# Macaron block on one core: where POOL issues the gathers of the expert stage, and what they wait for

## Chip, core and metric

One Trainium2 chip, one core. The metric is the time of one execution on the device in microseconds (us). The engines are PE (matrix products), DVE (vector), ACT (activations), POOL (GpSimd) and SP (SyncE, which here only issues DMAs); each runs its own instructions in order, and they wait for one another through semaphores.

## What is computed

Input x is 8 x 512 tokens of 128 floats. The block is a macaron: half a mixture-of-experts layer, attention, half a mixture-of-experts layer again.

```python
x = x + 0.5 * ffn(layernorm(x))          # pass 1
x = x + attention(layernorm(x))          # 16 heads, softmax, projection, residual, layernorm
x = x + 0.5 * ffn(layernorm(x))          # pass 2

def ffn(x):                              # 4096 tokens, 64 experts, top 8, at most 64 tokens an expert
    probs = softmax(x @ router_w.T)
    topk_w, topk_ids = top_k(probs, 8);  topk_w /= topk_w.sum(-1)
    # x_buf[e, c] = the c-th token that chose expert e (tokens past 64 are dropped)
    h = silu(x_buf @ w_gate) * (x_buf @ w_up)
    y = h @ w_down
    routed = segment_sum(y[slot] * topk_w, token)
    shared = (silu(x @ ws_gate) * (x @ ws_up)) @ ws_down
    return routed + shared
```

## The kernel before

The 4096 tokens are 32 tiles of 128 (NT), taken in 8 groups of 4 (NG = 8, GT = 4). Each pass of the mixture layer is one call of `ffn(f)` on every engine (f.p is 0 in pass 1 and 1 in pass 2), and runs through these stages.

**Routing.** Per group the tokens are normalised, the router's product is made, and the weights of the top 8 experts are computed. Rows of the normalised token and its 64 weights (192 floats) go to DRAM (`dispatch_rows`); the waits `xns` and `ws` are for these stores.

**Shared expert.** Per group PE makes the up products, ACT copies them, POOL multiplies them (`shared_mul`, L589 to L593), PE makes the down product, ACT copies it (`shy`), and DVE adds it to x in place (`shared_add`, L859, semaphore `shx`). SP stores the sum to DRAM, group by group (`store_base`, L406, semaphore `base`): this is the base to which the experts' outputs are added.

**Lists.** DVE finds for each expert its tokens, in two halves: the first 32 slots of all 64 experts while the shared expert runs, the second 32 slots in between steps 0 to 3 of the expert loop (`merge_blocks`, `open_blocks`, `top_tokens`, `indices`). SP stores each list (L410) and loads it back spread over all partitions (L414), in eight parts.

**Experts.** 16 steps q, each with two tiles of 128 slots (k = 2q and 2q + 1; one tile is the 32 slots of four experts). POOL gathers the 128 rows of a tile with an indirect DMA (`gather(k)`, L599) into one of 16 buffers; PE transposes them (`slots_t`), makes the gate and up products (`gate_up`, semaphore `gu`), transposes the hidden values (`hidden_t`), makes the down product (`down_e`), and in `sums` adds up rows of the same token within the step. DVE finds which slots hold the same token (`match`), picks the routing weights (`pick`), multiplies gate and up (`hidden`, L914) and copies the sums out of PSUM (`sum_copy`, L922, semaphore `smc`). POOL then adds the sums to the base in DRAM with two indirect DMAs (L626, "scatter" below, semaphore `sca`).

Three rules of order matter here. A pair of scatters starts when both the sums are copied and the pair before has landed. `sum_copy(q)` waits until the pair of step q - 2 has landed. And a gather into a buffer used before waits until its transposes and its `pick` are done (k at 16 or more).

POOL's order before: the shared products of groups 0 to 5, gathers 0 and 1, the product of group 6, gather 2, the product of group 7, gathers 3 to 5, then waits for all base stores and for the second gate and up product (`wait(pool, f.gu, 2)`, L616), gathers 6 to 9, and then step by step a pair of scatters and the gathers up to `ahead(q + 1)`, where `ahead(q)` is 10 + 2q, at most 32.

SP's order in pass 1: the stores of the weights mixed with the 24 loads of expert weights, 13 loads of the attention's weights (`attention_weights`), the first list's store and first load, eight base stores, then the other list loads, each when the transposes have come so far (`gtp`). In pass 2 no weights are loaded. POOL waits for the attention's weights after it has cleared buffers behind the last scatter of pass 1.

Of the kernel before, what the change touches and what calls it, by code (L numbers as in the profile page):

```python
# [15 lines left out]
def macaron_kernel(nc, x_in, wq, bq, wk, bk, wv, bv, wo, bo, gamma, beta,  # L16
# [13 lines left out]
    NP2 = E // 2  # L30
# [31 lines left out]
    with ExitStack() as ctx:  # L62
# [292 lines left out]
        def _(sp):  # L355
# [6 lines left out]
            def attention_weights():  # L362
                sp.dma_start(wv_sb[:], wv).then_inc(s_watt, 16)
                sp.dma_start(wo_sb[:], wo.rearrange("(j d) n -> d j n", d=HD)).then_inc(s_watt, 16)
                for i, (w, b) in enumerate(((wq, bq), (wk, bk))):
                    sp.dma_start(wqk_raw[:, i * D:(i + 1) * D], w).then_inc(s_watt, 16)
                    sp.dma_start(bqk_sb[:, i:i + 1], b.rearrange("(j d o) -> d j o", d=HD, o=1), allow_slow_non_contiguous=True).then_inc(s_watt, 16)
                for jj in range(4):
                    sp.dma_start(bv_sb[jj * 32:(jj + 1) * 32, :].rearrange("p (k d) -> p k d", k=4),
                                 bv.rearrange("(o k jj d) -> jj o k d", o=1, k=4, jj=4)[jj].to_broadcast([32, 4, HD]))\  # L370
                      .then_inc(s_watt, 16)
                for t, b in ((bo_sb, bo), (gamma_sb, gamma), (beta_sb, beta)):
                    sp.dma_start(t[:], b.rearrange("(o c) -> o c", o=1).to_broadcast([P, D])).then_inc(s_watt, 16)
# [6 lines left out]
            def ffn(f):  # L380
# [6 lines left out]
                if f.p == 0:  # L387
                    for g in range(NG):
                        if g:
                            store_w(g - 1, (g - 1) % 2)  # L390
                        expert_weights(2 * g)
                        expert_weights(2 * g + 1)
                    store_w(NG - 1, 1)
                    for c in range(2 * NG, 24):
                        expert_weights(c)
                    attention_weights()
                else:
                    store_w(0, 0)
                    with sp.Fori(1, NG // 2) as i:
                        for r in range(2):  # L400
                            store_w(2 * i + (r - 1), 1 - r)
                    store_w(NG - 1, 1)
# [16 lines left out]
                for g in range(NG):  # L419
                    store_base(g, g % 2)  # L420
                for c in range(1, 4):
                    wait(sp, f.gtp, 2 * c - 1)
                    load_rows(c)
                store_list(1)
# [94 lines left out]
        def _(pool):  # L519
# [40 lines left out]
            def ffn(f):  # L560
# [43 lines left out]
                for r in range(2):  # L604
                    wait(pool, f.xns[r], 16 * (NG // 2))
                    wait(pool, f.ws[r], 16 * (NG // 2))
                for k in range(2):
                    gather(k)
                shared_mul(NG - 2, 0)
                gather(2)  # L610
                shared_mul(NG - 1, 1)
                for k in range(3, 6):
                    gather(k)
                for r in range(2):
                    wait(pool, f.base[r], 16 * (NG // 2))
                wait(pool, f.gu, 2)  # L616
                ahead = lambda q: min(NP2, 10 + 2 * q)
                for k in range(6, ahead(0)):
                    gather(k)
                for q in range(NQ):  # L620
                    wait(pool, f.row, q + 1)
                    wait(pool, f.smc, q + 1)
# [93 lines left out]
        def _(dve):  # L716
# [18 lines left out]
            def ffn(f):  # L735
# [191 lines left out]
                top_blocks(1)  # L927
                for g in range(5, NG):
                    shared_add(g)
                match(0)  # L930
                pick(0)
                hidden(0)
                match(1)
                pick(1)
                for q in range(NQ):
# [302 lines left out]
        def _(pe):  # L1238
            def ffn(f):
# [124 lines left out]
                      .then_inc(f.sm.sem, 1)  # L1364

                wait(pe, f.shc, NG)
                wait(pe, f.shy, NG)
                slots_t(0)
                gate_up(0)
                slots_t(1)  # L1370
                hidden_t(0)
                for q in range(NQ):
                    if q + 1 < NQ:
# [163 lines left out]
```

## Time and profile before

| | us |
|---|---|
| median of 3 runs | 892.09 |
| lowest and highest | 890.61, 896.19 |
| the profiled execution | 889.63 |
| its span in the trace | 887.9 |

The page of that execution gives these busy times in its span: PE 680.9 us (77%), DVE 604.6 (68%), ACT 464.8 (52%), POOL 391.1 (44%). They are averages over stages: the attention lies in the middle and keeps PE and DVE busy, the mixture layer stands before and behind it. A row of a timeline has the start in us from the span's start, the duration in us, the engine, the line of the kernel, the operation, what it writes and reads, how many instructions are merged in the row, and in brackets how long the engine had been idle and what released it. The duration of an indirect DMA on POOL is the time in which POOL makes its descriptors; the data land later. Where an instruction waits for several semaphores, the releaser named is the one that the profile saw last and can be another than the one that held it.

### The profile page before, as it was taken

The page shows a single profiled execution, that of the slowest core. Times are in us where ns is not written, and L with a number is a line of the kernel's source. Part 1 is how long each engine was busy: PE and PEld are TensorE (multiplying, and loading weights), DVE is VectorE, ACT ScalarE, POOL GpSimd, SP SyncE. Part 2 cuts the span into 40 slices and gives each one's busy share as a digit, 9 for nine tenths or more (in the row PEclk, how much of TensorE's full clock was granted, in tenths as well). Part 3 has the DMA queues.
Part 4 walks back from the last instruction along what each step waited for, and adds up shares of the span by engine and source line. Part 5 has one row for each costly group of instructions (what it writes and reads, how often), then busy time and mean ns, then how long its engine had stood idle before and what let it go on. Part 6 is the DMA issues. An engine that isn't in the chain of part 4 may idle for free. (4 is left out here: it accounts for less than half of the span.)

```text
span 887.9 us, 17088 instructions
## 1 busy us (share of the span) xinstructions
PE 680.9 (77%) x5121; PEld 313.0 (35%) x5121; DVE 604.6 (68%) x1572; ACT 464.8 (52%) x1060; POOL 391.1 (44%) x509
## 2 busy tenths in 40 slices
PE   4876765703899999999999999999980289676650
PEld 3643443502133333333333333333210264354440
DVE  4868643344978888888888888888913669864420
ACT  5733232201177777777777777777772675323210
POOL 5545887676432332322322322321004745677762
PEclk9987577555599999999999999999995559757665
DMA  6996443243525444445445445445110131644334
GB/s 186 256 240 174 79 76 58 38 91 67 97 50 96 89 88 95 87 86 95 85 88 95 83 90 95 81 92 95 38 36 18 36 89 25 170 83 77 50 33 107
DMA packets 233724, 80.26 MB, mean 90 GB/s; under 512 B 166888, under 2 KB 226440, under 8 KB 233608
## 3 DMA queue, kind: packets, MB, share of 16 engines
q1 hardware_dynamic: 212936, 64.94, 33.6%
q0 software_dynamic: 12288, 10.49, 8.0%
q10 hardware_dynamic: 8448, 4.20, 1.6%
q8 instruction: 25, 0.41, 0.2%
q14 instruction: 27, 0.22, 0.1%
HBM read 49.94 MB, written 31.49 MB: 92 GB/s over the span
## 5 line engine op out<-in xcount | busy, mean ns | idle before, releaser
L987 DVE TENSOR_REDUCE arena<-psum 128x2 f32<-128x1024 f32 x256 | 308.8, 1219 | 53.2 <-PE psum L1434 50.2
L1206 ACT ACTIVATE arena<-psum 128x512 f32<-128x512 f32 x512 | 282.1, 600 | 116.3 <-PE psum L1447 114.8
L1434 PE MATMUL psum<-arena 126*128 126x512 bf16 x512 | 200.1, 398 | 4.0 <-DVE arena L987 3.2
L1447 PE MATMUL psum<-arena 128*128 128x512 bf16 x512 | 196.8, 387 | 7.3 <-ACT arena L1206 3.3
L1456 PE MATMUL psum<-arena 128*32 128x512 f32 x1024 | 136.2, 604 | 0.3
L682 POOL CAST arena<-arena 128x256 bf16<-128x256 f32 x32 | 12.7, 397 | 265.0 <-issue 261.0
L626 POOL DMA_INDIRECT sums<-sums_sb,sidx x64 | 103.3, 1614 | 42.0 <-DVE sums_sb L922 18.6
L1447 PEld LDWEIGHTS psum<-arena 128*128 128x128 bf16 x512 | 50.7, 100 | 150.2 <-ACT arena L1206 122.3
L599 POOL DMA_INDIRECT arena<-dispatch_rows,arena x64 | 66.3, 1036 | 33.2 <-issue 17.4
L922 DVE COPY sums_sb<-psum 128x256 f32<-128x256 f32 x32 | 13.6, 424 | 97.0 <-DMA sums<-sums_sb,sidx 78.1
L1434 PEld LDWEIGHTS psum<-arena 126*128 126x128 bf16 x512 | 49.6, 99 | 37.9 <-DVE arena L987 15.1
L1319 PE MATMUL psum<-ident,arena 128*128 128x128 f32 x64 | 22.0, 390 | 34.9 <-DMA arena<-dispatch_rows,arena 33.1
L1244 PE MATMUL psum<-ident,xn_sb 128*128 128x128 f32 x64 | 17.8, 433 | 39.1 <-ACT xn_sb L1083 39.1
L1329 PE MATMUL psum<-wgu_sb,arena 128*32 128x192 f32 x512 | 41.7, 467 | 0.9 <-ACT arena L1144 0.9
L1150 ACT ACTIVATE arena<-psum 128x192 f32<-128x192 f32 x32 | 10.6, 330 | 59.5 <-PE psum L1329 59.5
L1456 PEld LDWEIGHTS psum<-arena 128*32 128x32 f32 x1024 | 20.3, 108 | 53.6 <-issue 29.1
L1339 PE MATMUL psum<-ident,arena 128*96 128x128 f32 x64 | 18.5, 385 | 24.3 <-DVE arena L914 24.1
L1396 PE MATMUL psum<-ident,arena 128*128 128x128 f32 x32 | 11.2, 348 | 32.0 <-POOL arena L667 32.0
L1083 ACT ACTIVATE xn_sb<-x_sb,negm,rstd 128x128 f32<-128x128 f32 x64 | 26.4, 491 | 16.8 <-DVE negm L739 15.5
L1176 ACT ACTIVATE arena<-psum 128x128 f32<-128x128 f32 x32 | 8.7, 273 | 48.4 <-PE psum L1396 48.4
L1144 ACT ACTIVATE arena<-psum 128x256 f32<-128x256 f32 x32 | 12.3, 383 | 40.5 <-PE psum L1319 40.4
L1000 DVE RECIPROCAL arena<-arena 128x128 f32<-128x128 f32 x32 | 30.1, 942 | 4.3 <-DMA arena<-ctx 4.3
(138 smaller groups left out, 1115.6 us busy)
## 6 DMA issues: line engine op xcount, KB each, us to landing
arena<-qk_parts SPq DMA_DIRECT2D x128, 96.0 KB
ctx<-arena SPq DMA_DIRECT2D x32, 256.0 KB, 2.0
qk_parts<-arena SPq DMA_DIRECT2D x32, 192.0 KB, 3.8
dispatch_rows<-xn_sb ACTq DMA_DIRECT2D x16, 256.0 KB, 2.3
arena<-lists SPq DMA_DIRECT2D x16, 256.0 KB, 3.5
sums<-x_sb SPq DMA_DIRECT2D x16, 256.0 KB, 4.4
arena<-qk_parts SPq DMA_DIRECT2D x64, 64.0 KB
arena<-ctx SPq DMA_DIRECT2D x64, 64.0 KB, 2.5
```

What stands on the lines that cost most here:

```text
L599: pool.indirect_dma_start(out=gat[k % NGB], out_offset=None, in_=xw_dram[f.p], in_offset=bass.IndirectOffsetOnAxis(ap=gidx[:, k:k + 1], ax ...
L626: pool.indirect_dma_start(out=acc_dram[f.p], in_=sum_r[q % 2][:, j * D:(j + 1) * D], in_offset=None, out_offset=bass.IndirectOffsetOnAxis( ...
L987: dve.tensor_reduce(mx_r[r % 2][:, 2 * p:2 * p + 2], src, X, ALU.max).then_inc(a_mx, 1)
L1000: dve.reciprocal(den2_r[r % 2], den2_r[r % 2]).then_inc(a_rc, 1)
L1083: ins = act.activation(xn_sb[:, r, j, :], x_sb[:, t, :], ACT.Identity, scale=rstd[:, t:t + 1], bias=negm[:, t:t + 1])
L1206: act.activation(p_r[tau % NPB], bank[4 + tau % 2][:, :], ACT.Exp, scale=SCALE).then_inc(a_P, 1)
L1319: ins = pe.transpose(bank[0][:, j * P:(j + 1) * P], gat[k % NGB][:, 0:D], ident[:])
L1329: ins = pe.matmul(bank[2 + r][i * HC:(i + 1) * HC, j * 2 * F:(j + 1) * 2 * F], gT[r][:, j * P + i * HC:j * P + (i + 1) * HC], wgu_sb[:, e, :],
L1339: ins = pe.transpose(bank[4][0:F, j * P:(j + 1) * P], hid[r][:, j * F:(j + 1) * F], ident[:])
L1434: ins = pe.matmul(bank[tau % 4][:, :], heads(q_st[r], rows, g)[:, qt * P:(qt + 1) * P], heads(k_st[r], rows, g), start=True, stop=True)
L1447: pe.matmul(bank[4 + tau % 2][:, :], keys, heads(q_st[r], rows, g), start=True, stop=True)\
L1456: ins = pe.matmul(bank[6][32 * g:32 * g + 32, :], v_r[r][:, g, kt, :], p_r[(4 * kt + g) % NPB], start=(kt == 0), stop=(kt == 3), tile_posi ...
```

## The change

- POOL: gathers and the last two shared products alternate (gather 0, product 6, gather 1, product 7), and then gathers 2 to 15 follow in a row. The wait for the second gate and up product is gone. The wait for the base stores stands behind these gathers, ahead of the first scatter. `ahead(q)` becomes 8 + 2q, at least 16 and at most 32: steps 0 to 3 have no gathers behind their scatters, steps 4 to 11 have two each.
- SP: the attention's weights are loaded between the first and the second of the list loads that wait for transposes, not ahead of the first list's store.
- DVE: `hidden(0)` comes before `match(0)` and `pick(0)`.
- PE: the wait for the last copy of the shared output stands ahead of the first hidden transposes, not ahead of the first slot transposes.

```diff
@@ SP
                     for c in range(2 * NG, 24):
                         expert_weights(c)
-                    attention_weights()
@@ SP
                 for c in range(1, 4):
+                    if c == 2 and f.p == 0:
+                        attention_weights()
                     wait(sp, f.gtp, 2 * c - 1)
                     load_rows(c)
@@ POOL
-                for k in range(2):
-                    gather(k)
+                gather(0)
                 shared_mul(NG - 2, 0)
-                gather(2)
+                gather(1)
                 shared_mul(NG - 1, 1)
-                for k in range(3, 6):
+                ahead = lambda q: min(NP2, max(16, 8 + 2 * q))
+                for k in range(2, ahead(0)):
                     gather(k)
                 for r in range(2):
                     wait(pool, f.base[r], 16 * (NG // 2))
-                wait(pool, f.gu, 2)
-                ahead = lambda q: min(NP2, 10 + 2 * q)
-                for k in range(6, ahead(0)):
-                    gather(k)
@@ DVE
+                hidden(0)
                 match(0)
                 pick(0)
-                hidden(0)
                 match(1)
@@ PE
                 wait(pe, f.shc, NG)
-                wait(pe, f.shy, NG)
                 slots_t(0)
                 gate_up(0)
                 slots_t(1)
+                wait(pe, f.shy, NG)
                 hidden_t(0)
```

POOL's rows from the first six shared products (TENSOR_TENSOR of 96 x 512) into the expert loop; the DMA rows that read `dispatch_rows` are gathers, those that write `sums` are scatters. Before:

```order
L593 TENSOR_TENSOR arena<-arena 96x512 x6
L599 DMA arena<-dispatch_rows,arena 128x192 x2
L593 TENSOR_TENSOR arena<-arena 96x512
L599 DMA arena<-dispatch_rows,arena 128x192
L593 TENSOR_TENSOR arena<-arena 96x512
L599 DMA arena<-dispatch_rows,arena 128x192 x7
L626 DMA sums<-sums_sb,sidx 8448x128 x2
L599 DMA arena<-dispatch_rows,arena 128x192 x2
```

The same place in the changed kernel, where the lines have moved by a few numbers:

```order
L594 TENSOR_TENSOR arena<-arena 96x512 x6
L600 DMA arena<-dispatch_rows,arena 128x192
L594 TENSOR_TENSOR arena<-arena 96x512
L600 DMA arena<-dispatch_rows,arena 128x192
L594 TENSOR_TENSOR arena<-arena 96x512
L600 DMA arena<-dispatch_rows,arena 128x192 x14
L623 DMA sums<-sums_sb,sidx 8448x128 x10
L600 DMA arena<-dispatch_rows,arena 128x192 x2
```

Sixteen gathers stand ahead of the first scatter instead of ten, fourteen of them in a row, and the first five pairs of scatters follow one another with nothing between.

SP's rows in pass 1 behind the loads of expert weights; `lists` is the list in DRAM, `sums<-x_sb` the base stores. Before:

```order
L373 DMA gamma_sb<-in_L_attn_gamma 128x128
L373 DMA beta_sb<-in_L_attn_beta 128x128
L410 DMA lists<-arena 64x32
L414 DMA arena<-lists 128x512
L406 DMA sums<-x_sb 128x4x128 x8
L414 DMA arena<-lists 128x512 x3
```

In the changed kernel, from the last loads of expert weights on:

```order
L378 DMA wd_sb<-in_L_ffn_w_down 96x8x128 x8
L409 DMA lists<-arena 64x32
L413 DMA arena<-lists 128x512
L405 DMA sums<-x_sb 128x4x128 x8
L413 DMA arena<-lists 128x512
L363 DMA wv_sb<-in_L_attn_wv 128x128
L364 DMA wo_sb<-in_L_attn_wo 128x1x128
```

The list's store and the eight base stores stand ahead of the weights of the attention now, and two list loads stand behind them.

## Rows read from the trace of the kernel before

**Rows 1.** Groups by line: busy us, mean ns, then idle us before, with releasers.

```profile
L626 POOL DMA_INDIRECT sums<-sums_sb,sidx x64 | 103.3, 1614 | 42.0 <-DVE sums_sb L922 18.6 <-issue 15.8 <-DMA sums<-sums_sb,sidx 5.2
...
L922 DVE COPY sums_sb<-psum 128x256 f32<-128x256 f32 x32 | 13.6, 424 | 97.0 <-DMA sums<-sums_sb,sidx 78.1 <-PE psum L1363 18.8
```

**Rows 2.** Timeline of POOL, front of pass 1: L599 gather, L593 product, L626 scatter.

```profile
68.61 1.23 POOL L599 DMA_INDIRECT arena<-dispatch_rows,arena  x1 [0.30 <-issue]
...
71.30 0.99 POOL L599 DMA_INDIRECT arena<-dispatch_rows,arena  x1 [0.16 <-issue]
72.29 1.29 POOL L593 TENSOR_TENSOR arena<-arena 96x512 f32<-96x512 f32 x1
...
76.61 1.28 POOL L599 DMA_INDIRECT arena<-dispatch_rows,arena  x1 [0.30 <-issue]
85.92 0.94 POOL L599 DMA_INDIRECT arena<-dispatch_rows,arena  x1 [8.03 <-PE psum L1329]
...
90.93 1.63 POOL L626 DMA_INDIRECT sums<-sums_sb,sidx  x1 [0.30 <-issue]
```

**Rows 3.** Timeline of POOL, the same front in pass 2.

```profile
755.18 1.34 POOL L599 DMA_INDIRECT arena<-dispatch_rows,arena  x1 [0.31 <-issue]
...
758.99 1.28 POOL L593 TENSOR_TENSOR arena<-arena 96x512 f32<-96x512 f32 x1
...
769.67 0.94 POOL L599 DMA_INDIRECT arena<-dispatch_rows,arena  x1 [5.10 <-DVE pick L908]
...
774.67 1.91 POOL L626 DMA_INDIRECT sums<-sums_sb,sidx  x1 [0.30 <-issue]
```

**Rows 4.** Timeline of POOL: first scatter of steps 11 and 15, pass 1, pass 2.

```profile
163.72 1.62 POOL L626 DMA_INDIRECT sums<-sums_sb,sidx  x1 [0.30 <-issue]
...
187.79 1.55 POOL L626 DMA_INDIRECT sums<-sums_sb,sidx  x1 [2.56 <-DMA sums<-sums_sb,sidx]
...
848.64 1.63 POOL L626 DMA_INDIRECT sums<-sums_sb,sidx  x1 [0.30 <-issue]
...
873.54 1.55 POOL L626 DMA_INDIRECT sums<-sums_sb,sidx  x1 [2.96 <-issue]
```

**Rows 5.** Timeline of PE: second gate-and-up products; transposes and last sum products.

```profile
80.68 1.51 PE L1329 MATMUL psum<-wgu_sb,arena 128*32 128x192 f32 x16
...
138.13 0.47 PE L1319 MATMUL psum<-ident,arena 128*128 128x128 f32 x1 [0.73 <-DMA arena<-dispatch_rows,arena]
...
140.51 0.63 PE L1363 MATMUL psum<-arena 128*128 128x128 f32 x2
...
767.32 1.46 PE L1329 MATMUL psum<-wgu_sb,arena 128*32 128x192 f32 x16
```

**Rows 6.** Timeline of SP's DMA issues, pass 1: attention weights (first, last), last base store.

```profile
60.27 1.99 SPq L363 DMA_DIRECT2D wv_sb<-in_L_attn_wv  x1
...
68.28 0.43 SPq L373 DMA_DIRECT2D beta_sb<-in_L_attn_beta  x1
...
79.23 0.96 SPq L406 DMA_DIRECT2D sums<-x_sb  x1
```

**Rows 7.** From the answers on lines L406 (base stores) and L599 (gathers).

```profile
DMA to landing us min/median/max: 2.3/4.4/6.2
...
DMA to landing us min/median/max: 2.6/2.7/6.6
```

**Rows 8.** Timeline of DVE: an add of the shared output, sum copies of step 0, step 3.

```profile
76.38 0.69 DVE L859 TENSOR_TENSOR x_sb<-x_sb,z_sb 128x512 f32<-128x512 f32 x1 [0.89 <-ACT z_sb L1120]
...
84.64 0.42 DVE L922 COPY sums_sb<-psum 128x256 f32<-128x256 f32 x1 [1.67 <-PE psum L1363]
...
106.94 0.42 DVE L922 COPY sums_sb<-psum 128x256 f32<-128x256 f32 x1 [2.04 <-PE psum L1363]
...
793.55 0.42 DVE L922 COPY sums_sb<-psum 128x256 f32<-128x256 f32 x1 [2.04 <-PE psum L1363]
```

## Prediction

> **What bounds the kernel now.** I first read the grouped instructions for the two lines that POOL spends the expert stage on: 64 scatters (L626) of 1.61 us each, and on DVE the copy of the sums (L922), which works 13.6 us and stands idle 97.0 us, 78.1 of it until a scatter has landed [rows 1]. So in the expert stage DVE waits for POOL's scatters and not the other way round. I then read POOL's timeline in order of time. The stage runs twice (pass 1 before the attention, pass 2 after it), and both passes look alike: a **front**, from the last shared products to the first scatter [rows 2, 3], and a **loop** of 16 steps of two scatters each, with two gathers behind the pair as long as there are gathers left [rows 4]. Every step but a few begins 0.3 us after POOL's previous instruction, so the time of a pass is (start of the first scatter, call it T0) + 15 steps + a tail that the change leaves alone. The prediction is therefore two numbers for each pass: how T0 moves, and how the steps change. Nothing of the attention (it takes the middle of the span) is touched.
>
> The loop has two kinds of step. In pass 1 the eleven steps with gathers run from 90.93 [rows 2] to 163.72 [rows 4], 72.79 / 11 = 6.62 us each; the four without run from there to 187.79, 24.07 / 4 = 6.02 us. In pass 2: (848.64 - 774.67) / 11 = 6.72 us and (873.54 - 848.64) / 4 = 6.22 us [rows 3, 4]. A step without gathers is not shorter by the two gathers' 2.6 us, since a scatter must wait for the pair before it to land: a gather in the loop fills a wait that is there anyway, and taking a pair of gathers out of a step saves only 0.60 us (pass 1) or 0.50 us (pass 2).
>
> In the front POOL stands idle: 8.03 us before 85.92 in pass 1, 5.10 us before 769.67 in pass 2 [rows 2, 3]. Which of the two removed or moved waits held it? The second gate-and-up product (two of them are awaited, L616) ended at 80.68 + 1.51 = 82.19 in pass 1, 3.7 us before POOL went on, but at 767.32 + 1.46 = 768.78 in pass 2, 0.9 us before [rows 5]. The last base store of pass 1 was issued at 79.23, and such a store lands 4.4 us later in the median, 6.2 at most [rows 6, 7]: 83.6 to 85.4. So in pass 1 the base stores ended the wait (whatever releaser the row names), in pass 2 the product did.
>
> **The change, part by part.**
>
> *Front of pass 1.* One gather fewer stands ahead of the last shared product: the one of 68.61, 1.23 us and its gap of 0.30. The product moves from 72.29 to 70.76 and ends at 72.05 (it takes 1.29) [rows 2]. Then come 14 gathers with no wait. Of their pitch the trace has two prices: 1.25 us (the four from 85.92 to the scatter at 90.93: 5.01 / 4) and 1.58 us (the one of 76.61: 1.28 + 0.30) [rows 2]. The slow ones stand where DVE adds the shared output to x (L859, such an add at 76.38 [rows 8]); two of the 14 will again lie beside adds, and I count one more for the DVE work that POOL used to sit out. The first gather starts 0.16 after the product and takes 0.99, as the one of 71.30 did. T0 = 72.05 + 0.16 + 0.99 + 0.30 + 3 x 1.58 + 10 x 1.25 = 90.7, against 90.93: -0.2 us. The idle 8.03 us are filled by six more gathers, which cost about as much. That is the heart of it: the removed wait is spent on the moved work.
>
> *Front of pass 2.* The same count, but only 5.10 us of idleness to fill. The gather of 755.18 (1.34 + 0.31) is no longer ahead, so the product goes from 758.99 to 757.34 and ends at 758.62; T0 = 758.62 + 0.16 + 0.99 + 0.30 + 4.74 + 12.50 = 777.3, against 774.67 [rows 3]: **+2.6 us**.
>
> *Loop.* Gathers now go with steps 4 to 11 (8 steps), not 0 to 10 (11 steps). Three steps change kind: 3 x 0.60 = -1.8 us in pass 1, 3 x 0.50 = -1.5 us in pass 2.
>
> *Can the data keep up with T0 and the shorter first steps?* A scatter needs the copied sums of its step. The first were copied at 84.64 in pass 1, 5.8 us before the new T0. The tightest is step 3, behind the second list's top-token search on DVE: copied at 106.94 and 793.55, taking 0.42 [rows 8], against new scatter starts of 90.7 + 3 x 6.02 = 108.8 and 777.3 + 3 x 6.22 = 796.0. Between 1.4 and 2.0 us are left, so this adds nothing. Were it late, each us of lateness would be a us of the pass.
>
> *Base stores awaited by the scatters alone.* 0 us by itself: they land by 85.4 at the latest even if nothing else moved, over 5 us before T0.
>
> *Attention weights later (pass 1 only).* Their 13 transfers hold SP's queue from 60.27 to 68.28 + 0.43, 8.4 us [rows 6]. Ahead of them in the new order come the first list store, its load and the eight base stores, which become earlier by up to those us; behind them the loads of list rows 2 and 3, which DVE takes up for step 4 only shortly before its copy at 106.94 [rows 8]. Who waits for the weights starts after the last scatter, past 187.79. Cost 0; without that cover the list loads would stand behind 8.4 us.
>
> *The up-down order of the first hidden product, and PE's later wait for the shared output.* PE starts its first transposes some 1 to 2 us sooner, DVE takes hidden(0) before match(0) and idles for it instead. Both sit inside the 5.8 us before T0: 0 us.
>
> *Gathers one step later.* From step 4 on the gathers of a stage are issued after the pair four stages ahead of it, not five. In the trace PE already waits for each gather: it starts on the second half of a stage at 138.13, after a DMA wait, and then runs the hidden transposes and the three sum products, the last pair at 140.51 for 0.63 [rows 5]. That is 3.0 us from the landed gather to finished sums, plus 0.4 for the copy and 0.3 to 0.9 until POOL starts. The second gather starts 5.1 us after its pair of scatters (2 x 1.91 us for the pair, 1.3 for the first gather) and lands 2.7 us later in the median [rows 7]. Together 5.1 + 2.7 + 3.0 + 0.4 + 0.9 = 12.1 us, and the scatter that needs it is two steps on, 2 x 6.4 = 12.8 us at the least. So it just fits and costs 0, with 0.7 us or a little more to spare where before there was a whole step more.
>
> Sum: -0.2 + 2.6 - 1.8 - 1.5 = -0.9 us. The profiled execution took 889.63 us, so 888.7 us of that kind; it lies 2.5 us under the median of 892.09, and on the median's scale the forecast is **891.2 us**: no change that a measurement can tell.
>
> **Rivals.** (1) *Slow gathers throughout, ending slower.* If most of the 14 gathers run at the 1.58 pitch because DVE is busy beside them, 10 more cost 0.33 each, 3.3 us a pass: +5.7 in all, 897.8 us (891.2 + 6.6). For it: every gather beside an add is slow. Against it: the four from 85.92 ran beside DVE's top-8 and match work and took 1.25. It decides the sign from three slow gathers more than I count. The Trainium skill (SBUF — State Buffer, "SBUF: two separate sides") has a rule that speaks for this rival: a DVE instruction with two SBUF inputs and a GpSimd instruction that reads SBUF exclude each other on a shared port pair, and while GpSimd is locked out it can't write a DMA's descriptors. The slow row beside an add agrees with it. Taken at its word the rule covers the matches too (two SBUF inputs each), and the time would be that of this rival; the rows at 1.25 don't show that. (2) *Late gathers, ending clearly slower.* If a gather of the loop lands more than about 0.7 us late, the chain above sets the steps. At the longest landing seen, 6.6 us [rows 7], it would be 3.9 - 0.7 = 3.2 us over two steps, 1.6 us on each of 8 steps in two passes: +26 us at the worst; a constant 1 us of lateness above the spare gives 0.5 x 16 = +8, 899 us. (3) *The early steps don't shorten*, because list loads, weights and 14 gathers crowd their landings: the -3.3 is lost, +2.4 in all, 894.5 us. (4) *A gain after all*: with fewer DMAs among them the remaining gather steps fall towards the 6.44 us or so that POOL's own instructions take (two scatters of 1.61 and two gathers of 0.99 [rows 1, 2], with four gaps of 0.30: 6.40 to 6.44): 8 x 0.18 + 8 x 0.28 = -3.7 more, 887.5 us.
>
> **How the numbers follow.** My forecast 0.50; rival 1 0.17; rival 2 0.08; rival 3 0.13; rival 4 0.12. The low end is rival 4 with all gathers at 1.25 (another -2 us), 885.5; the high end takes in rivals 1 and 3 and a mild case of 2, 898.5. Measurements of this kernel tell about 1% (8.9 us) from no change. Faster than that no case reaches: 0.02. Slower by over 1% is the stronger half of rival 2: 0.05. Within 1%: 0.93.
>
> **What would show it.** In the profile of the changed kernel: 14 gathers in a row without idleness between them; T0 near 90.7 and 777.3; four steps of 6.0 to 6.2 us at the start, then eight of 6.4 to 6.7; DVE's sum copies released by PE rather than by a scatter's landing in steps 6 to 13, yet POOL never waiting for them. Wrong would be: POOL idle before the scatters of steps 6 to 13 (rival 2), T0 past 92.5 and 779 (rival 1), early steps of 6.6 us (rival 3).

## The result and the profile after

The changed kernel took **904.47 us** (median of 4, 903.2 to 905.8) against 892.73 us for the kernel before beside it (median of 4, 890.6 to 896.2): ratio 1.0137, 95% interval 1.0114 to 1.0160. It is 11.7 us slower; the prediction had 891.2 and a range up to 898.5, and the measured time lies beyond it. The experiments then showed a second result: in three later sittings (a sitting is one stretch of runs on one chip, with the kernel before timed beside every kernel) the same program was *faster* than the kernel before, by 0.2 to 0.45%, and in one it was again 1.4% slower. Both have to be explained.

The groups that answer to [rows 1] are in the first fence (busy us, mean ns, idle us before and releasers). POOL's idleness ahead of the scatters grew from 42.0 to 72.3 us, and DVE's copies of the sums are released by PE now (87.0 us of their idle time), where before a landed scatter released them (78.1).

```profile
L623 POOL DMA_INDIRECT sums<-sums_sb,sidx x64 | 101.6, 1587 | 72.3 <-DVE sums_sb L919 24.5 <-DMA sums<-sums_sb,sidx 21.2 <-issue 19.8
...
L919 DVE COPY sums_sb<-psum 128x256 f32<-128x256 f32 x32 | 13.6, 425 | 92.5 <-PE psum L1360 87.0 <-DMA sums<-sums_sb,sidx 5.4
```

POOL's timeline after, pass 1 (L600 gather, L623 scatter), and the end of the same front in pass 2. The row of 14 gathers runs without a gap and would have let the first scatter start at 88.05 + 1.25 = 89.3; it starts at 95.65, 6.66 us later than POOL was free [rows 2]. In pass 2 the same 6.71 us are lost [rows 3].

```profile
71.53 0.99 POOL L600 DMA_INDIRECT arena<-dispatch_rows,arena  x1 [0.16 <-issue]
...
75.32 1.18 POOL L600 DMA_INDIRECT arena<-dispatch_rows,arena  x1 [0.30 <-issue]
76.81 0.94 POOL L600 DMA_INDIRECT arena<-dispatch_rows,arena  x1 [0.30 <-issue]
...
88.05 0.94 POOL L600 DMA_INDIRECT arena<-dispatch_rows,arena  x1 [0.30 <-issue]
95.65 1.64 POOL L623 DMA_INDIRECT sums<-sums_sb,sidx  x1 [6.66 <-DVE sums_sb L919]
103.33 1.56 POOL L623 DMA_INDIRECT sums<-sums_sb,sidx  x1 [4.15 <-DVE sums_sb L919]
...
781.32 0.94 POOL L600 DMA_INDIRECT arena<-dispatch_rows,arena  x1 [0.30 <-issue]
788.97 1.63 POOL L623 DMA_INDIRECT sums<-sums_sb,sidx  x1 [6.71 <-DVE sums_sb L919]
```

What it waited for is found by going back engine by engine. PE's timeline after: L1326 are the first and the second gate and up product (steps 0 and 1), L1346 the down product, L1316 the transposes of step 2, L1336 the hidden transposes of step 1.

```profile
74.67 1.51 PE L1326 MATMUL psum<-wgu_sb,arena 128*32 128x192 f32 x16 [0.47 <-issue]
...
77.95 1.51 PE L1326 MATMUL psum<-wgu_sb,arena 128*32 128x192 f32 x16
79.23 1.08 PE L1346 MATMUL psum<-wd_sb,arena 96*32 96x128 f32 x16
80.24 0.69 PE L1316 MATMUL psum<-ident,arena 128*128 128x128 f32 x2
92.42 0.66 PE L1336 MATMUL psum<-ident,arena 128*96 128x128 f32 x2 [11.49 <-DVE arena L911]
```

ACT's timeline after: L1147 are the silus, of step 0 at 76.52 and of step 1 at 91.65, and L1155 is the copy of the hidden transposes of step 0. The silu of step 1 needs only the product that ended at 79.46.

```profile
76.52 0.33 ACT L1147 ACTIVATE arena<-psum 128x192 f32<-128x192 f32 x1 [1.91 <-PE psum L1326]
...
78.06 0.38 ACT L1155 ACTIVATE arena<-psum 96x256 f32<-96x256 f32 x1 [0.41 <-PE psum L1336]
91.65 0.33 ACT L1147 ACTIVATE arena<-psum 128x192 f32<-128x192 f32 x1 [13.21 <-remote]
...
784.88 0.33 ACT L1147 ACTIVATE arena<-psum 128x192 f32<-128x192 f32 x1 [11.01 <-remote]
```

DVE's timeline after: the multiplication of gate and up (L911) and the first copy of the sums (L919).

```profile
92.01 0.35 DVE L911 TENSOR_TENSOR arena<-arena,psum 128x192 f32<-128x192 f32 x1 [10.42 <-ACT arena L1147]
94.40 0.42 DVE L919 COPY sums_sb<-psum 128x256 f32<-128x256 f32 x1 [2.04 <-PE psum L1360]
```

So the second silu starts 12.2 us after its product has ended, with ACT idle for 13.21 us, and the first copy of the sums comes at 94.40 where it came at 84.64 [rows 8]. The release has no releaser by name ("remote"), and it comes 3.6 us after the start of the last gather of the row in both passes (88.05 to 91.65, 781.32 to 784.88). The update events of the semaphores in the trace say the same: the signals of the three PE groups above, which as a rule follow their ends by 0.01 to 0.06 us, come 12.2, 11.5 and 10.9 us late, in one burst from 91.63 to 91.83. They are not late from the start of the row, which begins at 71.53: the first product of the loop ended at 76.18 and its silu started at 76.52, 0.34 us later, and the copy at 78.06 followed its transposes (which ended at 78.02) at once. The long lateness sets in behind that, when seven of the row's fourteen gathers have started. In pass 2 it sets in sooner, with two signals of step 0 about 2 us late before the one of 12.15 us. DVE then runs the second list's search that much later, and the first four steps take 123.63 - 95.65 = 28.0 us, not 24.1.

### The profile page after: what moved, and what is told of

Its sections match the earlier page's. It is cut to its first block and busy times, and to the rows that moved or that the text cites. A ratio compares the mean times of both kernels' runs of the same rounds, so it can differ in the third digit from the quotient of the medians.

```text
span 901.5 us, 17025 instructions
## 1 busy us (share of the span) xinstructions
PE 678.6 (75%) x5060; PEld 311.9 (35%) x5121; DVE 607.1 (67%) x1572; ACT 461.6 (51%) x1060; POOL 387.3 (43%) x509
## 5 line engine op out<-in xcount | busy, mean ns | idle before, releaser
L1444 PE MATMUL psum<-arena 128*128 128x512 bf16 x451 | 173.3, 387 | 7.1 <-ACT arena L1203 3.3
L623 POOL DMA_INDIRECT sums<-sums_sb,sidx x64 | 101.6, 1587 | 72.3 <-DVE sums_sb L919 24.5
L919 DVE COPY sums_sb<-psum 128x256 f32<-128x256 f32 x32 | 13.6, 425 | 92.5 <-PE psum L1360 87.0
L600 POOL DMA_INDIRECT arena<-dispatch_rows,arena x64 | 64.2, 1003 | 20.6 <-issue 18.1
L1147 ACT ACTIVATE arena<-psum 128x192 f32<-128x192 f32 x32 | 10.6, 330 | 88.4 <-PE psum L1326 50.7
L1316 PE MATMUL psum<-ident,arena 128*128 128x128 f32 x64 | 24.2, 416 | 34.7 <-DMA arena<-dispatch_rows,arena 33.5
L1336 PE MATMUL psum<-ident,arena 128*96 128x128 f32 x64 | 18.0, 377 | 41.7 <-DVE arena L911 40.2
L1326 PE MATMUL psum<-wgu_sb,arena 128*32 128x192 f32 x512 | 43.1, 479 | 0.9 <-issue 0.5
L1134 ACT ACTIVATE arena<-psum,pick 128x128 f32<-128x128 f32 x64 | 20.0, 363 | 40.1 <-remote 25.8
L1393 PE MATMUL psum<-ident,arena 128*128 128x128 f32 x32 | 11.2, 348 | 29.5 <-POOL arena L664 29.5
```

Source lines behind the costliest of these rows:

```text
L600: pool.indirect_dma_start(out=gat[k % NGB], out_offset=None, in_=xw_dram[f.p], in_offset=bass.IndirectOffsetOnAxis(ap=gidx[:, k:k + 1], ax ...
L623: pool.indirect_dma_start(out=acc_dram[f.p], in_=sum_r[q % 2][:, j * D:(j + 1) * D], in_offset=None, out_offset=bass.IndirectOffsetOnAxis( ...
L1134: act.activation(y_r[r][:, j * D:(j + 1) * D], bank[1][:, j * D:(j + 1) * D], ACT.Copy, scale=pick_r[r][:, j:j + 1]).then_inc(f.ys.sem, 1)
L1316: ins = pe.transpose(bank[0][:, j * P:(j + 1) * P], gat[k % NGB][:, 0:D], ident[:])
L1326: ins = pe.matmul(bank[2 + r][i * HC:(i + 1) * HC, j * 2 * F:(j + 1) * 2 * F], gT[r][:, j * P + i * HC:j * P + (i + 1) * HC], wgu_sb[:, e, :],
L1444: pe.matmul(bank[4 + tau % 2][:, :], keys, heads(q_st[r], rows, g), start=True, stop=True)\
```

## The experiments

T0 is the start of the first scatter of a pass, T15 that of the first scatter of its last step (step 15); "events" are the semaphore updates recorded in the whole trace.

| trace | sitting | pass 1 T0, T15 | pass 2 T0, T15 | events |
|---|---|---|---|---|
| before, as shown | ? | 90.93, 187.79 | 774.67, 873.54 | 13,644 |
| after, the result | 1 | 95.65, 193.56 | 788.97, 886.54 | 12,339 |
| before once more | 4 | 88.71, 186.15 | 774.11, 872.57 | 13,669 |
| after, 2nd | 3 | 90.14, 183.85 | 773.19, 868.18 | 13,677 |
| after, 3rd | 4 | 89.00, 184.17 | 775.95, 871.03 | 13,695 |
| after, 4th | 5 | 88.56, 184.49 | 774.41, 869.42 | 13,663 |
| after, 5th | 6 | 95.48, 194.77 | 791.55, 890.75 | 12,325 |
| silu held | 4 | 94.39, 192.80 | 787.68, 886.06 | 13,718 |
| ten ahead, 2nd | 5 | 85.39, 184.74 | 768.66, 869.16 | 13,717 |
| ten ahead, 3rd | 7 | 87.86, 187.06 | 773.91, 875.21 | 12,448 |

**First comparison (sitting 2, the kernel before at 888.6 us): what brings the late silu?** Theory A: the unbroken row of gathers alone. Theory B: the new order on DVE and PE. Four kernels, each the changed one with one thing taken back.

The removed wait put back, in the middle of the row:

```diff
                 for k in range(2, ahead(0)):
+                    if k == 6:
+                        wait(pool, f.gu, 2)
                     gather(k)
```

> The changed kernel with one wait put back: ahead of gather 6 POOL waits for the second gate-and-up product, as the kernel before did; all 16 gathers stay ahead of the first scatter. In the changed kernel ACT starts the second silu of each pass some 12 us after PE has finished the product (91.65 against 79.46 us in pass 1), just when the last gather of the row has landed. Theory A (the unbroken row of gathers on POOL holds up what the other engines see of PE): the second silu comes within 0.5 us of the product again, since the row is broken there; POOL then issues ten gathers in a row, 12.5 us from about 80.4, and either the first sum copy is made before that row bites (at about 85) and the first scatter starts at 93, or the silu of step 2 or 3 is now the late one and the first scatter comes at 94 to 96 as in the changed kernel. Time 894 to 903. Theory B (the new order on DVE and PE, hidden(0) first and the later wait for the shared output, makes the silu late): no difference, the second silu stays at about 91, time 904.

892.3 us, 1.0052 (1.0034 to 1.0070), just under the 894 to 903 of the forecast. Ten gathers still followed the wait, T0 was 92.49.

Ten gathers ahead, without the wait:

```diff
-                ahead = lambda q: min(NP2, max(16, 8 + 2 * q))
+                ahead = lambda q: min(NP2, 10 + 2 * q)
```

> The changed kernel with the old reach of the gathers (10 + 2q): ten ahead of the first scatter, eight of them in a row, two more behind every pair from step 0 on; no wait for the product, all else as changed. Theory A (unbroken row): the row ends at about 81.8 in pass 1 (eight gathers at 1.25 to 1.3 from 71.5), so PE's products are seen late by at most some 4 us instead of 12; first sum copy at 84 to 87, first scatter at 86 to 88, before the 90.9 of the kernel before; time 886 to 891. Theory B (order on DVE and PE): second silu late as in the changed kernel whatever the row, first scatter near 95, time 903 to 906.

886.8 us, 0.9973 (0.9954 to 0.9993). T0 85.84, set by the first sums (copied at 84.60).

DVE's and PE's orders as before:

```diff
-                hidden(0)
                 match(0)
                 pick(0)
+                hidden(0)
@@
                 wait(pe, f.shc, NG)
+                wait(pe, f.shy, NG)
                 slots_t(0)
                 gate_up(0)
                 slots_t(1)
-                wait(pe, f.shy, NG)
```

> The changed kernel with DVE's and PE's order as before (hidden(0) behind match(0) and pick(0); PE waits for the shared output ahead of the first transposes); the 14 gathers in a row stay. Theory A (unbroken row): the late silu stays, until the row has landed (about 91.6 in pass 1); time 903 to 906. Theory B (order): the late silu is gone, first scatter at about 90, time 888 to 892.

886.6 us, 0.9975 (0.9963 to 0.9987), first sums at 83.35, T0 88.66.

At most three gathers in flight:

```diff
+                    if k >= 4:
+                        wait(pool, f.gat[k - 3], 16)
                     gather(k)
```

> The changed kernel where each gather k from 4 to 15 of the row first waits until gather k - 3 has landed, so that at most three are in flight. A gather lands about 2.7 us after its start and the pitch is 1.25 us, so the waits hold POOL little: the row gets perhaps 0.2 to 0.5 us longer per gather, with short gaps of waiting. Theory A1 (what matters is that POOL never waits within the row): PE's products are seen on time, first sum copy at about 84 to 86, first scatter at 92 to 95 for the longer row. Theory A2 (what matters is the number of gathers issued in one stretch, waiting or not): the second silu is late as in the changed kernel, until the row has landed. Theory C (too many gathers in flight, their landings crowd something out): gone as well, so A1 and C would need another run.

892.7 us, 1.0052 (1.0027 to 1.0077), T0 93.67. In none of the four was the second silu late. Read alone, the four seem to support theory B, with the length of the row mattering too. That reading was unsound: the changed kernel itself was not run beside them.

**Second comparison (sitting 3, before at 888.2): the halves of theory B, and the changed kernel itself.**

> The changed kernel once more, unaltered, on the chip of these comparisons. Earlier 904.5 us, 1.0137 times the kernel before. Theory A (the late silu belongs to this program: a long row of gathers together with the new order on DVE and PE): the second silu again starts some 12 us behind its product in pass 1 and 12 us in pass 2, the first sum copies at 94 and 788, the time 1.012 to 1.016 times before, here 899.5 to 903. Theory C (the lateness is a chance of that execution or of that chip): the second silu within 1 us of its product, first sum copies at 83.4 to 84.6, time 886 to 892.

**886.3 us, 0.9982 (0.9966 to 0.9998).** No late silu, first sums at 83.79. Theory B fell with this run: the unaltered kernel does without the lateness whatever the order. With DVE's half taken back:

> The changed kernel, with DVE's order as before (match(0), pick(0), hidden(0)); PE's later wait for the shared output stays. The run with both undone took 886.6 us. If hidden(0) ahead of match(0) is the half that brings the lateness: 885.5 to 888, second silu within 1 us of its product. If PE's wait is the half: 898 to 903, second silu 12 us late. If only the phase of PE's first products against the row of gathers counts, either half undone will do: 885.5 to 888 here too, and the same in the run with PE's half undone.

886.1 us, 0.9980 (0.9962 to 0.9998). With PE's half taken back:

> The changed kernel, with PE's wait for the shared output ahead of its first slot transposes as before; DVE's new order stays. If PE's half brings the lateness: 885.5 to 888, second silu within 1 us of its product. If DVE's half brings it: 898 to 903. If the phase alone counts: 885.5 to 888 both here and with DVE's half undone.

887.8 us, 0.9995 (0.9977 to 1.0014). With both taken back and ten gathers ahead (the two diffs above together):

> The changed kernel with both orders as before and ten gathers ahead of the first scatter instead of sixteen (two behind each pair from step 0 on), still without the wait for the second gate and up product. Ten ahead alone took 886.8 us, with T0 at 85.84 and 772.01 set by the first sum copy at 84.60 and 770.67; with the old orders the first sum copy came at 83.35. Theory: T0 follows the sum copy, 1.2 us earlier in each pass, and the loop stays as it is: 886.8 - 2.4 = 884.4 us, the fastest so far. Rival: the second list's search on DVE sets steps 1 and 3 and follows the sum copy too, so the same; or the old order costs DVE as much as it gives, then 886.8.

886.2 us, 0.9984 (0.9965 to 1.0003): T0 did come sooner in pass 1 (84.88), but the time is that of its neighbours, and the forecast of 884.4 missed; where the rest went was not followed up. All four lie within 1.7 us: neither order is worth anything that can be seen here.

**Third comparison (sitting 4, before at 888.2): is the late silu enough for the loss?** On ACT, in the changed kernel:

```diff
                     if q + 1 < NQ:
+                        if q == 0:
+                            wait(act, f.gat[15], 16)
                         silu(q + 1)
```

> The changed kernel with one wait more: on ACT the second silu (step 1) waits until the last of the sixteen gathers has landed, in both passes. The changed kernel took 904.5 us when its second silu was late by itself and 886.3 us when it was not. If the whole of that difference comes from this one late silu: first sum copies near 95 and 776, T0 near 96 and 778, four first steps of some 28 us instead of 24.3 because the second list's search on DVE is pushed back too, together +8 to +10 us in each pass: 902 to 906 us. If the late silu was only one sign of something that also slowed the rest of the execution: no more than the +6 us or so by which T0 moves in each pass, 896 to 899 us.

902.4 us, 1.0159 (1.0139 to 1.0179); beside it the unaltered kernel and a trace of the one before:

> The changed kernel unaltered, a third time. If the late second silu depends on the chip or on how the program was placed, it comes in all executions of a sitting or in none: either 0.996 to 1.000 times the kernel before with first sum copies at 84 and 767, or 1.012 to 1.016 times with 94 and 788. If it comes by chance from execution to execution, the times of this sitting are mixed.

884.9 us, 0.9955 (0.9942 to 0.9968).

> The kernel before, unaltered, for a trace from the same chip as its neighbours. It was 892.7 us beside the first result and 888.2 to 888.6 us in the later comparisons. If that difference of 4 us lies in the same stretch as the late silu, its front has shorter waits than the trace of before: first scatters earlier than 90.9 and, counted from the first gather of the pass, earlier than 21.1 us in pass 2. If it is the chip, the difference is spread over the whole span.

888.8 us, with T0 of pass 1 at 88.71 where the trace shown has 90.93, and of pass 2 774.11 - 753.00 = 21.1 us behind the first gather, as there. Where a disturbed sitting costs the kernel before its 4 us no trace shows, since this one and the one shown both have all their events.

Holding one silu back until the sixteenth gather has landed costs 17.5 us and gives the T0 and T15 of the result to about 1.3 us (table). ACT's timeline, the second silu held, then that of the unaltered kernel in the same sitting:

```profile
90.39 0.33 ACT L1147 ACTIVATE arena<-psum 128x192 f32<-128x192 f32 x1 [12.80 <-DMA arena<-dispatch_rows,arena]
```

```profile
79.39 0.33 ACT L1147 ACTIVATE arena<-psum 128x192 f32<-128x192 f32 x1 [1.09 <-PE psum L1326]
```

POOL's timeline of that unaltered kernel: the row ends, the scatter follows at once, as forecast.

```profile
87.75 0.95 POOL L600 DMA_INDIRECT arena<-dispatch_rows,arena  x1 [0.30 <-issue]
89.00 1.64 POOL L623 DMA_INDIRECT sums<-sums_sb,sidx  x1 [0.30 <-issue]
...
94.91 1.56 POOL L623 DMA_INDIRECT sums<-sums_sb,sidx  x1 [2.38 <-DMA sums<-sums_sb,sidx]
```

**Fourth comparison (sitting 5, before at 888.5): does it come back, and what length is best?**

> The changed kernel unaltered, a fourth time, with shorter rows of gathers beside it in the same sitting. Either 0.995 to 0.999 times the kernel before (884 to 887 us), first sum copies at 84 and 768; or, if the late silu is back, 1.012 to 1.016 times. Two of three sittings so far were without it, so about one chance in three that it is back.

887.0 us, 0.9979 (0.9967 to 0.9992). Ten ahead in the same sitting:

> Ten gathers ahead instead of sixteen, nothing else changed, a second time (886.8 before). Where the changed kernel beside it has no late silu: the same within 2 us of it. Where it has: if the unbroken row of fourteen is needed for the lateness, this one stays at 885 to 888; if any row of gathers shows it in such a sitting, the second silu waits until the tenth gather has landed, near 85 in pass 1, about 5 us late, and the time is 3 to 8 us longer.

885.2 us, 0.9957 (0.9935 to 0.9979). Twelve ahead:

> Twelve gathers ahead of the first scatter, two behind each pair from step 0 to 9. The twelfth gather ends before the first sums are copied (84 to 85), so T0 stays where ten ahead has it (85.8), and one step less has gathers than there: -0.5 us in each pass, 885.8 us against 886.8. Rival: the step behind the first pair waits for a landing that twelve gathers push back, as after the sixteen (6.7 to 8.4 us in pass 2), then it is the same as ten ahead or 1 us worse.

889.3 us, 1.0000 (0.9985 to 1.0016). Both forecasts failed, for a reason that POOL's timeline of this kernel shows:

```profile
102.65 1.58 POOL L623 DMA_INDIRECT sums<-sums_sb,sidx  x1 [0.30 <-issue]
109.35 1.02 POOL L600 DMA_INDIRECT arena<-dispatch_rows,arena  x1 [5.12 <-DVE arena L850]
```

Twelve ahead brings gather 16, the first of the second half of the lists, behind step 2. L850 writes that half's row numbers, and POOL stood 5.12 us for it: step 2 took 11.24 us in both passes. With ten ahead that gather comes in step 3, with sixteen in step 4.

**Fifth comparison (sitting 6, before at 892.6).**

> The changed kernel unaltered, a fifth time. Without the late silu 884 to 888 us, 0.995 to 0.999 times the kernel before; with it 1.012 to 1.016 times. Three of four sittings were without it.

**905.8 us, 1.0141 (1.0108 to 1.0174).** The late silu is back. The second silu starts at 91.48 in pass 1, T0 is 95.48: both within 0.2 us of the result's. The weights in their old place:

```diff
                     for c in range(2 * NG, 24):
                         expert_weights(c)
+                    attention_weights()
@@
-                    if c == 2 and f.p == 0:
-                        attention_weights()
```

> The changed kernel with the attention's weights loaded where they were, ahead of the first list's store. My theory (they cost nothing in either place): the same as the changed kernel beside it within 1 us. Rival: in the old place they hold back the first list's load and the base stores, which 14 gathers no longer cover; the base stores then land near 85 still, ahead of the first scatter at 89 to 90, but the first gathers start up to 1 us later: +1 us. A gain from the old place: the gathers of pass 1 no longer share the queue with them, -1 us.

904.0 us, 1.0111 (1.0080 to 1.0142). The intervals of the two overlap, so the difference of 1.7 us is not clear of the noise, which leaves room for some 4 us to either side of it. The traces are closer: the first gather starts at 65.68 with the weights in the old place and at 65.70 in the new one, T0 of pass 1 is 95.11 against 95.48. Ten ahead with the silu held:

> Ten gathers ahead of the first scatter (two behind each pair from step 0 on), and the second silu held until the tenth gather has landed. Unheld it took 885.2 and 886.8 us. The tenth gather starts near 81.4 in pass 1, so it has landed near 85.0; the first sum copy follows the silu by 2.8 us, 87.8 instead of 84.6, and T0 and the scatters of steps 1 and 3, which follow the sum copies, move by the same 3.2 us: +6.4 in both passes, 892 us. With the row of fourteen the hold cost 17.5 us. Rival: the scatters take up slack in the loop and it costs under 3 us.

892.8 us, 1.0002 (0.9978 to 1.0027): 892 was forecast for an otherwise undisturbed execution. The trace shows that it wasn't: the product's own signal was 3.8 us late, 0.8 us short of the hold. So the hold added only that, and the match with 892 is in part luck. Beside it in this sitting, the signal behind the row of fourteen was 12.3 us late. That gave the forecast for the last kernel.

**Sixth comparison (sitting 7, before at 890.9): ten ahead, nothing held.**

> Ten gathers ahead, nothing else changed, a third time. In a sitting of the kind without late signals (the kernel before at 888 to 889 us): 885 to 887 us, ratio 0.996 to 0.998. In a sitting with them (the kernel before at 892 to 893 us): the second silu waits until the row of ten is over, at about 84.2 in pass 1 as its product's signal did in the held run, so 0.8 us earlier than held in each pass: about 891 us, ratio 0.998 to 1.000. Rival there: the signals are late at several places of the loop too, then 893 and more.

891.0 us, 0.9992 (0.9973 to 1.0011), as forecast for a disturbed sitting. PE's and ACT's timelines of this kernel: the product ends at 79.82, the silu starts at 83.87.

```profile
78.31 1.51 PE L1326 MATMUL psum<-wgu_sb,arena 128*32 128x192 f32 x16
```

```profile
83.87 0.33 ACT L1147 ACTIVATE arena<-psum 128x192 f32<-128x192 f32 x1 [5.07 <-remote]
```

Its row of gathers ends sooner, and so does the lateness. POOL's timeline of the same kernel:

```profile
80.86 0.95 POOL L600 DMA_INDIRECT arena<-dispatch_rows,arena  x1 [0.30 <-issue]
87.86 1.63 POOL L623 DMA_INDIRECT sums<-sums_sb,sidx  x1 [6.05 <-DVE sums_sb L919]
```

The release comes 3.0 us after the last gather's start here, 3.6 us in the result, and 2.7 to 3.7 us in pass 1 of the five disturbed traces (gathers land 2.7 us after their start in the median [rows 7]). The long lateness so ends about when the row's last gather lands: it is 4.0 us with the tenth gather as the last, 12.2 us with the sixteenth.

The signals are late further on in the loop too, by less. In the same kernel, the down product of PE (L1346) ends at 116.25, its signal is recorded at 118.46, and ACT's instruction that needs it (L1134) starts then:

```profile
115.49 0.76 PE L1346 MATMUL psum<-wd_sb,arena 96*32 96x128 f32 x16
```

```profile
118.48 0.62 ACT L1134 ACTIVATE arena<-psum,pick 128x128 f32<-128x128 f32 x2 [1.99 <-remote]
```

Counted over both expert stages of the result's trace, 34 of PE's 160 recorded signals come more than 0.2 us behind the end of their product, 21 of them more than 1 us. In the other four disturbed traces it is 31 to 60 of some 155. In the fifteen undisturbed ones none of some 170 does, and the latest is 0.14 us behind. Where POOL's own work sets the steps of the loop, a signal 2 us late costs little; the one behind the row meets the first sums, for which everything waits.

**What is shown.** There are two kinds of sitting. In three of seven (1, 6 and 7) PE's signals to the other engines come late in the expert stages, where POOL works through gathers and scatters, and latest behind a long row of gathers; in four they don't. (The changed kernel itself was not run in sittings 2 and 7; the traces of its relatives tell the kind there.) The kind held for every execution of the changed kernel in its sitting (4 and 2 of them at 903 to 906.5 us, 10, 8 and 9 at 882 to 889.1). In the disturbed kind the changed kernel loses 904.5 - 886 = 18.5 us, ten ahead 891.0 - 886 = 5 us, and the kernel before 892.7 - 888.4 = 4.3 us (2.5 in sitting 7). Ratios within a sitting so hide a part of the loss: the result's 11.7 us are the 18.5 less the 4.3 that the kernel before lost there too and less the 2.3 by which the change gains in undisturbed sittings.

That one late silu is enough for nearly all of the loss is shown by the held silu, 17.5 of 18.5 us. That the length of the row sets how late it is rests on five disturbed traces with two lengths, both of them in sitting 6. What makes a sitting disturbed is not shown. Nor is it shown that the removed wait would have helped: it was put back only in an undisturbed sitting, no trace of the kernel before fell in a disturbed one, and ten ahead, without the wait, takes as long as the kernel before in sitting 7 (0.9992). So the runs speak for the length of the row and not for the wait by itself.

## Why the prediction was wrong, point by point

*T0 of pass 1, 90.7.* In undisturbed sittings 90.14, 89.00 and 88.56, right to about 2 us; against the kernel before in sitting 4 (88.71) that is +0.5 in the mean, where -0.2 was forecast; against the trace that the forecast was made from (90.93) it is -1.7. In the result 95.65.

*T0 of pass 2, +2.6 us.* Counted from T15 of pass 1, before 774.11 - 186.15 = 587.96; after 589.34, 591.78, 589.92: +2.4 in the mean. Against the trace that the forecast was made from (774.67 - 187.79 = 586.88) it is +3.5. Right to about 1 us. In the result 595.41.

*The pitch of the row, and rival 1.* Right: of the 14 gathers of pass 1 one took 1.18 us, all others 0.94 to 0.99. Three slow ones had been counted. The shared-port rule of the Trainium skill (SBUF — State Buffer, "SBUF: two separate sides") that spoke for this rival shows at most in that one: it starts at 75.32, and DVE's adds run from 74.39 to 76.29. Beside the matches, from 77.16 on, the gathers took 0.94 to 0.95 us, so this trace does not agree with the rule there.

*Loop, -1.8 and -1.5.* From T0 to T15 before 97.44 and 98.46 (sitting 4), after 94.9 and 95.0 in the mean of three: -2.5 and -3.4. Undersized in pass 2, where a part of rival 4 came true: the eight gather steps of the third trace took (853.30 - 800.58) / 8 = 6.59 us each, against 6.72 before [rows 3, 4].

*Late gathers, rival 2.* False: ahead of the scatters of steps 6 to 12 POOL is idle for 0.3 to 1.5 us in the third trace; before, where the gathers end a step sooner, for 0.3 to 1.6 us ahead of those of steps 6 to 11. Most of the sum copies are released by PE, as said (two of the eight of steps 6 to 13 in pass 1 by a landing).

*Base stores and attention weights at 0.* Nothing speaks against it. The weights' place was tested only in a disturbed sitting and only to some 4 us, the base stores not by themselves.

The sum of -0.9 us was thus about right for the undisturbed kind: measured -1.9, -3.3 and -1.6 us. The loop gave 2.6 us more than forecast, and T0 of pass 1 took 0.7 of it back.

**The step that failed** stands in the part on DVE and PE, and again in the part on whether the data keep up: "The first were copied at 84.64 in pass 1, 5.8 us before the new T0" and "Both sit inside the 5.8 us before T0: 0 us" (by its own numbers, 90.7 - 84.64 - 0.42, the room is 5.6 us). It took for granted that PE's signals reach ACT and DVE at once whatever POOL does, and that the removed `wait(pool, f.gu, 2)` only kept POOL waiting. In a disturbed sitting the sums are copied at 94.40, 9.8 us later, since the signals of step 1 came only with the end of the 14 gathers. The term that was put at 0 costs twice in each pass: against the mean of the three undisturbed traces, T0 of the result is 6.4 us late in pass 1 and 5.1 in pass 2 (counted from T15 of pass 1), and the first four steps, which wait for the second list's search, take 3.2 and 2.9 us more. Together these are 17.6 of the 18.5 us. The old wait had split the row of gathers; whether that would have been enough in a disturbed sitting no run shows. No rival named this: all five forecasts kept the sums of step 0 where they were.

**A hint in the numbers was passed over.** The profiled execution (889.63 us) lay 2.5 us under the median, and below each of the three timed runs. Its trace has 13,644 events, close to those of undisturbed traces (13,663 to 13,729), and none of PE's signals in its expert stages is over 0.07 us late, so it is of the undisturbed kind, while 892.09 and 892.73 go with the medians of disturbed sittings. The prediction shifted its sum by the 2.5 us and asked no further.

## What to carry to other kernels

An unbroken row of descriptor work on one engine has a length that other engines can pay for. When a change makes such a row longer, ask who needs signals during it, and price the row at its full length for them; a wait that only splits the row deserves the same question before it is removed, though here its worth was not shown. Ten gathers ahead here gains as much as sixteen where nothing is disturbed (0.9957 and 0.9973 against 0.9955 to 0.9982) and loses 5 us where sixteen lose 18.5, so of the versions tried it is the one to keep. And run the changed kernel itself beside the experiments that are to explain it, in each sitting: four experiments here "cured" a lateness that their sitting didn't have.

## What was not expected of the hardware

The whole execution leaves fewer semaphore events in disturbed sittings: 12,325 to 12,480 in five traces of five, against 13,644 to 13,729 in the other fifteen. They are missing around the gathers and scatters, not in the attention: from 50 to 200 us the result has 470, 475 and 333 in stretches of 50 us, the third trace of the changed kernel 1,066, 637 and 541; from 300 to 600 us both have 880 to 960 each. DVE's are missing too: of the 16 that its instructions should have left between 78 and 91.5 us in the result, 3 are recorded, though DVE itself went on at once. The kernel with the silu held, which stands still just as long, has all of them (13,718), so the standstill is not what removes them. The granted clock does not tell the kinds apart (0.820 in the result, 0.825 with the silu held).

A matmul's end in the profile is not the moment at which others see it. The rows above have 12.2 us between the two. The Trainium skill (Perfetto Trace Analysis, "Tensor Engine Instruction (MATMUL, LD_WEIGHTS)") says that PE's end is estimated from the instruction's size, and that the semaphore update follows PSUM's acknowledgement and has still to propagate; the trace agrees, and gives the distance a size that the page doesn't.

Open: what makes a sitting disturbed. It isn't the chip as numbered, since sittings 3 and 6 were both on number 13. Whether PE's updates are late or their delivery could not be told apart. The Trainium skill (NOTIFIC — the notification-queue block, "7.1 Overflow: three behaviours, one of which stalls the engine") describes a path of trace records that, when it is full, loses records or holds up their producer, depending on how it is set. If both came together here, that would join the missing events to the late signals, and would mean that the recording itself takes part in the loss; every execution here was recorded, so no run shows or excludes it.
